# A gated slot attention layer with a feed-forward layer: slots written out, and work moved from VectorE to ScalarE and GpSimd

## What is computed

```python
q = short_conv(h @ Wq, cq); k = short_conv(h @ Wk, ck)     # 4 taps over time, then silu
v = short_conv(h @ Wv, cv); w = l2norm(short_conv(h @ Ww, cv))
g = log_sigmoid(h @ Wf1 @ Wf2); beta = sigmoid(h @ Wb)
def step(Sk, Sv):                                          # for each token, head by head
    Sk = Sk * exp(g) + k * (beta * w)
    Sv = Sv * exp(g) + (beta * w) * v
    a = softmax(q @ Sk * SCALE)
    return a @ Sv
o = o * rsqrt(mean(o * o) + EPS) * norm_w * sigmoid(h @ Wg1 @ Wg2 + bg2)
x = layernorm(x + o @ Wo)
x = layernorm(x + ffn(x))                                  # silu(x @ Wgate) * (x @ Wup) @ Wdown, int8 weights
```

## Time and profile before

| | |
|---|---|
| device time, median of 3 runs | 2336.53 us (2335.55 to 2337.49) |
| the profiled execution | 2341.29 us, its span 2339.6 us |
| busy: PE, PEld, DVE, ACT, POOL | 2040.0, 1652.6, 1966.1, 1208.3, 1114.0 us |
| mean granted TensorE clock | 0.956 of full speed |
| DMA | 9 GB/s over the span |

### The profile page before, as it was taken

How to read it: one execution, slowest core, us unless ns; L and a number is a source line. 1 busy time by engine, 2 the same in 40 slices (tenths; PEclk the granted TensorE clock), 3 DMA queues, 4 the chain that set the end, 5 groups by cost and what they waited for, 6 DMA issues and landing times.

```text
span 2339.6 us, 48157 instructions
## 1 busy us (share of the span) xinstructions
PE 2040.0 (87%) x12192; PEld 1652.6 (71%) x12192; DVE 1966.1 (84%) x4955; ACT 1208.3 (52%) x3359; POOL 1114.0 (48%) x1741
## 2 busy tenths in 40 slices
PE   7789899898989899898989899898989898997576
PEld 6577777677777777677777777677777677776465
DVE  1899889898989899898989899898989898995555
ACT  2455555555555556554555555555555555553322
POOL 4355545455444554445545454445545454544233
PEclk7899999999999999999999999999999999998688
DMA  2000000000000000000000000000000000000000
GB/s 56 1 11 5 10 4 10 7 6 11 5 12 5 10 4 13 5 8 10 5 12 5 12 5 9 5 10 7 5 13 5 12 5 10 4 5 1 16 18 18
DMA packets 41834, 21.82 MB, mean 9 GB/s; under 512 B 13744, under 2 KB 41520, under 8 KB 41520
## 3 DMA queue, kind: packets, MB, share of 16 engines
q1 hardware_dynamic: 41520, 18.10, 2.9%
HBM read 15.99 MB, written 2.10 MB: 8 GB/s over the span
## 4 chain that ended last, share of the span: by engine, by line
DVE 44%; issue 24%; PE 23%; POOL 3%; ACT 2%; DVEq 2%; DMA 1%; SPq 0%; POOLq 0%; ACTq 0%
DVE conv L473 12%; DVE U L458 5%; PE proj_ps L594 5%; DVE A L587 5%; DVE wT L466 4%; DVE tot L519 3%; DVE wT L483 3%; PE proj_ps L1246 3%; DVE V_ps L560 3%; DVE acc L540 2%; PE work_ps L708 2%; PE V_ps L649 2%; PE V_ps L627 2%; PE mix_ps L681 2%; ACT conv L346 2%
## 5 line engine op out<-in xcount | busy, mean ns | idle before, releaser
L473 DVE SCALAR_TENSOR_TENSOR conv<-proj_ps,coef,conv 128x511 f32<-128x511 f32 (+2 forms) x576 | 422.4, 733 | 64.1 <-ACT conv L346 59.5
L311 POOL TENSOR_TENSOR W<-W,tot 128x256 f32<-128x256 f32 x384 | 256.1, 667 | 368.7 <-PE mix_ps L681 363.1
L840 POOL TENSOR_TENSOR A_lev<-A,masks 128x256 f32<-128x256 f32 x448 | 332.9, 744 | 162.0 <-ACT A L375 162.0
L594 PE MATMUL proj_ps<-hT_hi,w_hi 128*128 128x512 f32 x512 | 238.5, 466 | 108.7 <-issue 47.7
L681 PE MATMUL mix_ps<-W,U 128*128 128x128 f32 x1792 | 309.4, 294 | 13.0 <-POOL W L311 6.3
L649 PE MATMUL V_ps<-A_lev,UT 128*128 128x128 f32 x1792 | 288.7, 284 | 31.7 <-DVE V_ps L560 31.6
L681 PEld LDWEIGHTS mix_ps<-W,U 128*128 128x128 f32 x1792 | 250.7, 191 | 59.9 <-POOL W L311 40.5
L649 PEld LDWEIGHTS V_ps<-A_lev,UT 128*128 128x128 f32 x1792 | 240.0, 191 | 61.0 <-issue 52.1
L587 DVE COPY_PREDICATED A<-masks,mix_ps 128x256 f32<-128x256 uint32 x448 | 269.1, 601 | 6.6 <-PE mix_ps L681 6.6
L390 ACT ACTIVATE UT<-tr_ps 128x512 f32<-128x512 f32 (+1 forms) x256 | 139.3, 544 | 172.8 <-PE tr_ps L618 170.7
L466 DVE TENSOR_TENSOR wT<-wT,tot 128x128 f32<-128x128 f32 x768 | 208.0, 313 | 14.8
(11 more groups left out here) (181 smaller groups left out, 4868.3 us busy)
## 6 DMA issues: line engine op xcount, KB each, us to landing
acc<-in_L_attn_hidden_states SPq DMA_DIRECT2D x1, 2048.0 KB, 8.4
w_raw<-in_L_attn_Ww SPq DMA_DIRECT2D x16, 128.0 KB, 3.0
w_raw<-in_L_attn_Wq SPq DMA_DIRECT2D x16, 128.0 KB, 2.2
w_raw<-in_L_attn_Wk SPq DMA_DIRECT2D x16, 128.0 KB, 2.3
w_raw<-in_L_attn_Wv SPq DMA_DIRECT2D x16, 128.0 KB, 2.1
wo_raw<-in_L_attn_Wo SPq DMA_DIRECT2D x16, 128.0 KB, 2.0
out_x<-acc SPq DMA_DIRECT2D x4, 512.0 KB, 2.9
wf_head<-in_L_attn_Wf SPq DMA_DIRECT2D x16, 64.0 KB, 1.9
```

What stands on the lines that cost most here:

```text
L311: nc.gpsimd.tensor_tensor(w, w, block_tot(u3.par, lev, 0), ALU.mult).then_inc(W_step, 1)
L473: nc.vector.scalar_tensor_tensor(y_, proj_ps[:, CONV_BANK[i], 0:T - back], filt(i, KW - 1 - back), y_, ALU.mult, ALU.add).then_inc(conv_st ...
L594: last = nc.tensor.matmul(dst, w[:, k, :], x_(k), start=(k == 0 and n == 0), stop=(k == KT - 1 and n == 2))
L840: nc.gpsimd.tensor_tensor(dst, diag_after_odd(lev), mask_cols(lev), ALU.mult)\
```

## The change

- All 67 slots are written out; no loop is left on any engine, wait values are constants, and the coefficients, `bg2_sb` and beta are read in place, so `coef`, `coef_v` and `gbias` go.
- The weights are split in three parts: w and q (512 columns) and k (256) of the next head in the last slot of a head (rounds 3 and 5 on ACT, behind `fac` on POOL), v (256) in the first slot of the new one.
- `gates` goes from DVE to ACT (round 0), `values` from DVE to ACT (round 2) as four scaled copies of 128x128.
- All seven `gate_products` go from DVE to POOL: levels 1 to 3 between the levels of `grow_W`, 4 to 7 behind `fac`.
- The sum over heads: ACT copies y times `rms` from PSUM to `y_sb` (rounds 6 and 7, four of 128x256), and POOL adds `y_sb` to `acc` (four additions of 128x256, two ahead of the last silu product and two behind it).
- The four squares of oN go to round 0 of the next slot on ACT, into a buffer of their own; the `rms` chain on POOL moves from ahead of the levels to behind the fifth.

```diff
+        self.edge = not 3 < off < units
+        self.next_h = off // 4 + 1 if off % 4 == 3 and off + 1 < units else None
-    with eng.Fori(1, heads) as h:
-        for j in range(seqs):
-            yield Slot(h, j, units)
+    for n in range(heads * seqs + 3):
+        yield Slot(n, heads * seqs)
...
+        W_PARTS = (slice(0, 2), slice(2, 3), slice(3, 4))
+        def high_weights(act, h, i):
+            for landed in ((head_w, head_q), (head_k,), (head_v,))[i]:
+                act.wait_ge(landed, 16 * (h + 1))
+            nc.scalar.activation(w_hi[:, W_PARTS[i]], w_raw[:, W_PARTS[i]], ACT.Copy).then_inc(high_done, 1)
+        def low_weights(pool, h, i):
+            pool.wait_ge(high_done, 3 * h + i + 1)
+            nc.gpsimd.tensor_tensor(w_lo[:, W_PARTS[i]], w_raw[:, W_PARTS[i]], w_hi[:, W_PARTS[i]].bitcast(F32),
+                                    ALU.subtract).then_inc(low_done, 1)
...
-        def gates(dve, u1):
-            nc.vector.tensor_scalar(gT[:, u1.par % 2, :], fexp[:, :], 0.5, 0.5, ALU.mult, ALU.add).then_inc(decay_step, 1)
+        def gates(act, u1):
+            nc.scalar.activation(gT[:, u1.par % 2, :], fexp[:, :], ACT.Copy, bias=0.5, scale=0.5).then_inc(gate_set, 1)
...
-            nc.vector.tensor_tensor(tot[:, u2.par, T - 2 * n:T - n], src[:, :, 0], src[:, :, 1], ALU.mult)\
+            nc.gpsimd.tensor_tensor(tot[:, u1.par, T - 2 * n:T - n], src[:, :, 0], src[:, :, 1], ALU.mult)\
                 .then_inc(decay_step, 1)
...
+            for c in range(C):
+                nc.scalar.activation(vN[:, u2.par % 2, c * P:(c + 1) * P], work_ps[:, 1, c * P:(c + 1) * P], ACT.Copy,
+                                     scale=fac[:, u2.par, c:c + 1]).then_inc(vN_done, 1)
+        def scale_output(act, u4, t):
+            nc.scalar.activation(y_sb[:, t, :], work_ps[:, t // 2, (t % 2) * HID:(t % 2 + 1) * HID], ACT.Copy,
+                                 scale=rms[:, u4.par % 2, t:t + 1]).then_inc(ys_done, 1)
+        def add_heads_output(pool, u4, t):
+            pool.wait_ge(ys_done, u4.count(4, t + 1))
             a = acc[:, u4.par * C + t, :]
-            nc.vector.scalar_tensor_tensor(a, work_ps[:, t // 2, (t % 2) * HID:(t % 2 + 1) * HID],
-                                           rms[:, u4.par % 2, t:t + 1], a, ALU.mult, ALU.add).then_inc(acc_done, 1)
+            nc.gpsimd.tensor_tensor(a, a, y_sb[:, t, :], ALU.add).then_inc(acc_done, 1)
...
+                if u4:
+                    add_heads_output(pool, u4, 0)
+                    add_heads_output(pool, u4, 1)
+                if u1:
                     silu_qk(pool, u1, 2)
+                if u4:
+                    add_heads_output(pool, u4, 2)
+                    add_heads_output(pool, u4, 3)
```

More of the change, by code:

```diff
@@ L167, in build @@
         oN = sb("oN", [P, T])
+        squares = sb("squares", [P, C, P])
         ssqo = sb("ssqo", [P, 2, C])
@@ L935, in _ @@
                     act.wait_ge(proj_ps_ready, u1.count(5, 2))
-                    wait(act, decay_step, u1.count(8, -7))
+                    wait(act, gate_set, u1.count(1, 0))
                     nc.scalar.activation(fexp[:, :], proj_ps[:, 1, :], ACT.Tanh, scale=0.5).then_inc(fexp_done, 1)
@@ L941, in _ @@
                         evac_UT(act, u2, (2, 2, 3, 3, 4, 5)[r])
+                    if u1 and r == 0:
+                        gates(act, u1)
+                    if u4 and r == 0:
+                        act.wait_ge(oN_done, u4.count(1, 1))
+                        for c in range(C):
+                            nc.scalar.activation(squares[:, c, :], oN[:, c * P:(c + 1) * P], ACT.Square,
+                                                 accum_out=ssqo[:, u4.par % 2, c:c + 1]).then_inc(osq_done, 1)
                     if u1 and r == 1:
                         tap(act, u1, 1)
+                    if u2 and r == 2:
+                        values(act, u2)
                     if u1 and r == 3:
@@ L964, in _ @@
                         tap(act, u1, 2)
+                    if s.next_h and r == 5:
+                        act.wait_ge(proj_ps_ready, u1.count(5, 4))
+                        high_weights(act, s.next_h, 1)
+                    if u4 and r in (6, 7):
+                        scale_output(act, u4, 2 * r - 12)
+                        scale_output(act, u4, 2 * r - 11)
                     if u2 and r == 7:
@@ L980, in _ @@
                     tanh(act, u1, 2)
-                if u3:
-                    act.wait_ge(oN_done, u3.count(1, 1))
-                    for c in range(C):
-                        nc.scalar.activation(unused_chunk(c), oN[:, c * P:(c + 1) * P], ACT.Square,
-                                             accum_out=ssqo[:, u3.par % 2, c:c + 1]).then_inc(osq_done, 1)
             act.wait_ge(ffn["q_in"], 48)
@@ L1041, in _ @@
             dve.wait_ge(const_ready, 4)
-            for s in slots(dve, H, B):
+            for s in slots(H, B):
                 u1, u2, u3, u4 = s.u1, s.u2, s.u3, s.u4
-                if u1 and s.j == 0:
-                    wait(dve, conv_step, u1.count(12, -3))
-                    wait(dve, tap_done, u1.count(4, -1))
-                    nc.vector.tensor_copy(coef[:, :, :], coefs[:, :, bass.ds(u1.h, 1), :].rearrange("p i o w -> p i (o w)"))\
-                        .then_inc(coef_set, 1)
                 if u3:
@@ L1087, in _ @@
                         silu_w(dve, u1)
-                    if u1 and r == 3:
-                        gates(dve, u1)
                     if u1 and r == 4:
@@ L1099, in _ @@
                         conv_tap(dve, u1, 1, 0)
-                    if u2 and r == 4:
-                        values(dve, u2)
                     if u1 and r == 4:
@@ L1200, in _ @@
             pe.wait_ge(beta_step, 2)
-            for s in slots(pe, H, B):
+            for s in slots(H, B):
                 u1, u2, u3, u4 = s.u1, s.u2, s.u3, s.u4
```

230 lines of the change are left out of this document (98 added, 132 removed).

## The result

The changed kernel takes 2435.94 us (median of 4 runs, 2432.28 to 2439.72) against 2336.04 us (2333.76 to 2337.49) before: a ratio of 1.0429 with an interval of 1.041 to 1.0447. It is 4.3% slower, where I forecast 2288 us and a range up to 2362. The profiled execution took 2436.33 us.

What follows compares the result with a forecast made beforehand. DVE was taken to bound part A and PE part B of each slot. 2341.3 - 6 (slots) - 44 (edges) + 1 (end) = 2292 us, 2288 as median; own range 2265 to 2310, 8-in-10 range 2235 to 2362.

Steps and rivals of the forecast that it cites:

- first rival: PE's pauses make the clock fall in two of three slots: 61 us, time 2350 us; chance 0.3.
- part A: From the turn of V to the gate product, set by DVE: 9.43 us before, about 10.5 us forecast.
- forecast of the pauses: PE idle about 0.7 us ahead of the turn of U_top and about 1.85 us more for the taps.
- price of a fallen slot: 3.4 us at half clock, worth 1.5 to 1.7 us, all in part B.
- part B: From the gate product to the next turn of V, set by PE: 22.12 us before, about 21.0 forecast, two pauses gone.
- written-out levels: Five levels of U in straight code, 0.93 us apart against 0.86, make part A 0.35 us longer.
- The additions: POOL's pair behind the silu product delays the first levels of U: 0.85 us in part A, bounds 0 and 1.4.
- second rival: POOL's additions block nothing that counts: part A 0.85 us shorter, 49 us less, 2239 us; chance 0.2.
- The pair ahead of the silu product: These additions fall into DVE's wait for the turn of V: no cost, or up to 0.5 us.
- DVE's gate products: Between U's levels in part A they fill time in which a copy waits anyway; removing them gains nothing.
- The edges: At each new head 4.8 us go, 72 us in all; 1.9 us come back, 28 us: net gain 44 us.
- `w_lo`: PE waiting for the weights' low part was named as a sign that the prediction is wrong.

Runs made afterwards that it cites:

- e5: Changed kernel with two and three extra matmuls of unused result in PE's pauses ahead of the turn of U_top and of the gate product: 2328.82 us.
- e7: Changed kernel with the two additions behind the last silu product kept there and the other pair moved one slot later, under DVE's taps: 2385.41 us.
- e9: Changed kernel with one wait more: the first level of W on POOL waits for U_top; 2349.3 us in one run.
- e6: Changed kernel with the sum over heads back on DVE, as in the kernel before the change: 2276.78 us.
- e11: e3 with only w's low part split ahead of the last silu product, q and k behind the additions in the next slot: 2229.17 us.
- e10: e3 with the waits ahead of the copy in U's growth reordered, so that the one met last in time stands last: 2273.16 us.
- e2: Changed kernel with POOL's four additions cut to one column of 256, all waits kept: 2237.63 us.
- e3: Changed kernel with all four additions one slot later, behind U_top and the first level of W, beside DVE's taps: 2234.85 us.
- e8: Changed kernel with the two additions ahead of the last silu product kept there and the pair behind it moved one slot later, under DVE's taps: 2244.91 us.
- e4: Changed kernel with four and seven extra matmuls of unused result in PE's pauses ahead of the turn of U_top and of the gate product: 2407.88 us.
- e12: e11 with the waits ahead of the multiplication in U's growth swapped and two extra products in PE's remaining pause for the taps: 2184.02 us.
- e1: The kernel before the change with its slots written out and nothing else changed: 2329.96 us.

## Why the prediction was wrong

**The step that failed is the choice between forecast and first rival**: whether the pauses of PE in part A make the clock fall. The sum put this at nothing; it cost 107 us (after against e5). I had seen the mechanism, its place and the point from which it decides, and gave it 0.30 because a pause of 1.5 us had left the clock at 1.00 and one of 3.3 had not the earlier trace rows. I took the two pauses apart. The runs show that they count together. From the waits of each run (mean idle time of PE ahead of the turn of U_top and ahead of the gate product) and the count of slots:

| kernel | part A | for U_top | for the taps | fallen of 60 | half clock, us |
|---|---|---|---|---|---|
| after | 10.93 | 1.20 | 1.77 | 56 | 266 |
| e7 | 10.84 | 1.28 in 49 slots | 1.73 | 44 | 218 |
| e9 | 10.46 | 0.66 | 1.81 | 31 | 106 |
| e6 | 9.67 | 0.6 in 16 slots | 1.69 | 16 | 55 |
| e11 | 9.49 | 0.3 in 5 slots | 1.80 | 13 | 44 |
| e10 | 9.87 | 0.34 in 46 slots | 1.79 | 12 | 41 |
| e2 | 9.89 | 0.6 in 27 slots | 1.77 | 6 | 20 |
| e3 | 9.49 | 0.3 in 2 slots | 1.71 | 4 | 14 |
| e8 | 9.50 | 0.6 in 5 slots | 1.70 | 2 | 7 |
| e4 | 12.34 | 0 | 0 | 0 | 0 |
| e5 | 10.93 | 0.36 | 0.55 | 0 | 0 |
| e12 | 9.16 | 0 | 0.77 | 0 | 0 |
| e1 | 9.80 | 0 | 1.05 in 49 slots | 14, at heads' edges | 51 |
| before | 9.42 | 0 | 0.72 | 15, at heads' edges | 78 |

Two of the rows behind it, of after and of e9:

```profile
PE proj_ps L1235 <- DVE conv L478: 111.6, 63, 1.9
...
PE tr_ps L631 <- DVE U_top L455: 74.1, 62, 1.6
```

```profile
PE proj_ps L1237 <- DVE conv L478: 113.8, 63, 1.9
...
PE tr_ps L631 <- DVE U_top L455: 41.2, 62, 1.0
```

With the pause for the taps alone 2 to 13 slots fall, with a second one of 0.7 us ahead of it half, with 1.2 us nearly all. A pause further off did not do the same: in e7 PE stands 1.66 us for aN in a head's first slots, some 4 us ahead of the turn of U_top, and 3 of these 15 fell, the three that also stood 0.6 us for U_top; of the other 45, with 1.3 us for U_top, 41 fell. Laid on the beat of the clock, as for e11, the 31 fallen gate products of e9 share one stretch of 1.8 us and the 56 of after one of 2.4, where those of e11 shared 0.3; none of the slots that kept the clock starts in it. A longer pause widens the stretch in which a slot falls, and how many hit it is left to how the slots come to lie on the beat: 4 or 13 at nearly equal pauses is chance (three of the 4 of e3 start in the 0.3 us of e11, and none of its other slots does).

My forecast of the pauses was 0.7 and 1.85 us, which is e9: there 31 slots fell and the one run took 2349.3 us, where the rival said 2350 (with 41 fallen slots). So with part A as I forecast it, the rival came true.

**The price of a fallen slot was right, their number was not.** I took 1.5 us for each and two of three slots, 61 us. One stretch of 3.4 us lengthens part B from 20.84 to 22.47, 1.63 us, and a second one in the same slot adds 0.87. But 78 stretches came, in 56 slots, and the whole measured 107 us (after less e5). The rival's time stopped at 2350, and the range at 2362, because I let two of three slots fall, and each once.

**Part A** was to be 10.5 us and was 10.93. Its terms: the written-out levels, 0.35 forecast, 0.38 measured (e1). The additions, 0.85 forecast for the pair behind the silu product, 0.97 measured (e3 to e9). These two were right, and the second rival (the additions block nothing) falls. The Trainium skill (SBUF — State Buffer, Who interferes with whom) says that a VectorE instruction with two SBUF inputs and a GpSimd instruction that reads SBUF exclude each other for a whole instruction. The trace agrees: 0.49 us of multiplications became 1.38 beside two additions, and the taps, with an input in PSUM, stayed at 2.31. The mis-sized term is one that I didn't have: the first level of W on POOL, which cost nothing before and came to lie beside the last level of U once DVE was late, 0.5 us. The pair ahead of the silu product, nothing or up to 0.5 us in the prediction, took nothing in two slots of four and 0.5 us in the other two, where a low part stands beside it (e8 against e3); in v's slot that is the step from 10.93 to 11.45.

A term goes the other way. 9.42 + 0.38 + 0.97 + 0.5 is 11.27, 0.34 us too much. Without additions in this place the changed kernel has a part A of 9.44 (e3), where the kernel before, written out, has 9.80 (e1): the change takes 0.36 us off, and I had 0.1. I had put DVE's gate products at nothing, since they fill waits. But the one behind the maximum didn't: in the slot of rows 5 it lay beside POOL's silu product and stood ahead of the copy,

```profile
1141.82 0.67 DVE L519 TENSOR_TENSOR tot<-tot 128x64 f32<-128x64 f32 x1
```

and the second copy behind the maximum starts 3.34 us behind the turn of V before, 3.41 in e1 and 3.08 in e3. That is read from the rows; no run takes this product away alone.

**Part B** was to be 21.0 us and is 20.84 at full clock, 1.3 us less than before. Both pauses went as said, and ACT's copies hold nobody; POOL holds PE three times a slot for 0.16 us, for W.

**The edges.** After, at full clock (e5), the first slot is 1.7 and the second 0.5 us longer than the rest (31.81), 2.2 us against 1.9 forecast. Before it was 4.2 us by the same means (35.85 + 31.30 less twice 31.46), against the 4.8 that I took. The net gain is then 2.0 x 15 = 30 us instead of 44. That PE didn't wait for `w_lo` was right.

**The sum again**, with what was measured at full clock (e5): slots inside a head 31.81 us against 31.46 before, 60 x 0.35 = 21 us lost where I forecast 6 gained; the edges 30 us gained; behind the last maximum 1 us gained (194.9 us against 195.9), where I forecast 1 lost. 2341.3 + 21 - 30 - 1 = 2331 us, where the profiled execution of e5 took 2332.1. Then the clock, 107 us, which makes 2438, where after took 2436.3. So without the clock the kernel would have taken 2329 us (the median of e5), 41 us over my 2288 and outside the forecast's own range of 2265 to 2310: part A and the edges were off as well, with the same sign.

## What to carry to other kernels

When an engine off the critical path gets work "beside" the critical one, ask for each instruction on the critical chain whether it shares a port with the new neighbour, and then which instruction that was harmless will meet the chain once it is late; the same four additions cost 94 us beside SBUF multiplications (e5 to e3) and nothing beside taps that read PSUM. Making VectorE's share shorter only helps where TensorE then waits less: add up all pauses of TensorE that lie near each other, since here the clock answered to them together, and if a pause can't be removed, a few products into an unused part of a bank can hold the clock, as long as they end before the wait does (2436 to 2329 us; with a longer fill, 2408).

## What of the hardware was not expected

- Two waits ahead of one DVE instruction are not alike. With the wait that is met last standing first, the copy started 0.53 us behind the multiplications' start, with it standing last 0.60; for the multiplication behind the copy 0.33 and 0.40. Over five levels and U_top this was 0.37 us of a slot one way (e10) and 0.28 the other (e12). The Trainium skill (Perfetto Trace Analysis, Identifying Dependency Chains) says that ahead of an instruction that waits on several engines, instructions of their own may be put in for the additional waits; no run here shows whether the time goes there. In the loop, whose waits are in registers, the waits of the multiplication stood in the slow order and it still came 0.33 us behind the copy; why is open.
- The clock did not follow the slot alone: in e11 slots with equal lengths and equal pauses fell or did not, 13 of 60, and in e3 with the same pauses 4. The changes of the clock keep a beat of their own, and whether a slot falls hangs on where its pause lies on it (0.3 us of it in e11, 2.4 us in after).
- One wait on POOL in front of an instruction that was not urgent (e9) was worth 87 us in this kernel, in a single run.
